# Graph attention scores: a2.W h taken from the W h product and spread by transposes, in place of a second product

## The chip, the cores and the metric

The kernel runs on one core of a Trainium2 chip. The core has five engines with instruction queues of their own that meet only in semaphores: PE (TensorE, matrix products and transposes into PSUM), DVE (VectorE), ACT (ScalarE), POOL (GpSimd) and SP (SyncE, DMA issue). The metric is the device time of one execution in microseconds; lower is better.

## The reference

A batch of 32 graphs with 256 nodes and 128 features passes two pre-norm blocks with residuals. The change is in the first, a graph attention layer:

```python
h = jnp.maximum(_layernorm(x, axis=-1), 0.0)
Wh = jnp.einsum('bnf,fo->bno', h, W)
a1, a2 = (a[:Fout, 0], a[Fout:, 0])
s1 = Wh @ a1
s2 = Wh @ a2
e = s1[:, :, None] + s2[:, None, :]
e = jnp.where(e >= 0, e, ALPHA * e)
e = jnp.where(adj_matrix[None] == 0, -jnp.inf, e)
attention = jax.nn.softmax(e, axis=-1)
h_prime = jnp.einsum('bij,bjo->bio', attention, Wh)
```

The second block (two graph convolutions, then LSTM steps over windows of 1 to 4 rows) is left as it is.

## The kernel before

Two graphs, four tiles of 128 nodes, make a pair; there are 16 pairs (`PAIRS`). Every engine has its own program, written by hand in a fixed order. In phase A, the attention layer, `ticks` calls `phase_a(t, ph, live)` once for each tick t on each engine, and `live(s)` holds where pair t - s exists; so a tick works on several pairs at different depths. I write q for pair t - 1 and give the steps short names:

- **W(q)**, PE L898: four products `hT` times `wext` into `psW`. `wext` holds 130 columns: 0.8 a1.W, the 128 columns of W, and -a1.W.
- **S(q)**, PE L902: one product of `wa2`, a 128x128 matrix whose columns are all a2.W, with `hT`: 512 columns in which every row holds a2.W h of each node. It goes to `psS` and signals `a_S`.
- **T(q+1)**, PE L908: four transposes of `v_norm` into `psT`.
- **A(q-3)**, PE L917: eight products of `pT` with `wh`, the attention's sum, into `psA`; signals `a_att`.
- **PT(q-2)**, PE L929: eight transposes of `prob` into `psPT`.
- ACT, in this order in a tick: `wh` (L467, the copy of `psW` out of PSUM, signals `a_wh`), `hT` (L474), `prob` (L481, four exponentials, which need `ebias`), `v_norm` (L448, four), `pT` (L490, the copy of `psPT`).
- DVE, in this order: a wait on `a_S`; `low` (L650) of pair q-1 and the first of four score passes of pair q over `psS` (L642); `ebias` (L654) of pair q-1; the other three L642; two `bn_stats` (L632); four score passes of pair q that take `wh`'s -a1 column (L674, signal `a_z`); the reciprocal of the attention's row sums (L681, waits on `a_att`); two more L632; four updates of `xs` (L688) of pair q-3, which signal `a_x1`.

`low` and `ebias` of pair q-1 do not read `psS`, but they stand behind the wait on `a_S` of pair q in DVE's program. A(q-2) overwrites `psA` and so waits on `a_x1` of pair q-3. In the first five ticks DVE also takes the statistics of x for later pairs (L594), and POOL (L357 to L366) turns them into the scale and shift that `v_norm` needs; `v_norm` of pair 6 waits for the last of these.

Phase B (graph convolutions) begins beside the last ticks of phase A; from then on PE runs mostly the products of L937, and the LSTM steps follow.

Of the kernel before, what the change touches and what calls it, by code (L numbers as in the profile page):

```python
# [5 lines left out]
def preln_gat_gcn_lstm_kernel(  # L6
# [24 lines left out]
    ALU = mybir.AluOpType  # L31
# [25 lines left out]
    with ctx:  # L57
# [25 lines left out]
        adj_neg = sb("adj_neg", [P, 2, N])  # L83
        adjT_hi = sb("adjT_hi", [P, 2, N], fp32r)
        adjT_lo = sb("adjT_lo", [P, 2, N], fp32r)
        wext = sb("wext", [P, D + 2])
        wa2 = sb("wa2", [P, P])
        wt = sb("wt", [P, D])
        a12 = sb("a12", [P, 2])
        wg_raw = sb("wg_raw", [P, 2, D])  # L90
# [27 lines left out]
        with ExitStack() as early:  # L118
            def sb_early(name, shape):
                return early.enter_context(nc.sbuf_tensor(name, shape, fp32))  # L120

            hT = sb_early("hT", [P, 512])
            score = sb_early("score", [P, 4, 4, N])
            prob = sb_early("prob", [P, 4, 4, N])
            pT = sb_early("pT", [P, 4, N])

            wh = sb_early("wh", [P, 4, 4, D + 3])
        h_hi = sb("h_hi", [P, NODES], fp32r)
        with ExitStack() as parts_end:
            h_lo = parts_end.enter_context(nc.sbuf_tensor("h_lo", [P, NODES], fp32r))  # L130
# [16 lines left out]

        ps = ctx.enter_context(nc.psum_tensor("ps", [P, 8, 512], fp32))
        psT = ps[:, 0, :]
        psW = ps[:, 1:3, 0:2 * (D + 2)]  # L150
        psS = ps[:, 3, :]
        psPT = ps[:, 4:6, :]
        psA = ps[:, 6:8, 0:2 * (D + 2)]
# [178 lines left out]
        def _(pool):  # L332
            n = 0

            def done(ins):
# [8 lines left out]
            done(nc.gpsimd.memset(ident[:, :], 0.0))  # L344
            nc.gpsimd.affine_select(out=ident[:, :], in_=ident[:, :], compare_op=ALU.not_equal, fill=1.0, base=0,
                                    pattern=[[-1, P]], channel_multiplier=1).then_inc(ident_ok, 1)
            nc.gpsimd.memset(wh[:, :, :, D + 2:D + 3], 1.0)
            nc.gpsimd.memset(ones[:, :].bitcast(fp32), 1.0).then_inc(ones_ok, 1)
            done(nc.gpsimd.memset(half[:, :], -0.5))

# [78 lines left out]
        def _(act):  # L429
            act.dma_start(wt[:, :], w_gat_t).then_inc(gat_w_in, 16)  # L430
            act.dma_start(a12[:, :], a_gat).then_inc(gat_w_in, 16)
            act.dma_start(wext[:, 1:D + 1], w_gat).then_inc(wext_in, 16)
            act.dma_start(adj_raw[:, :, :], adj.rearrange("(u p) n -> p u n", p=P)).then_inc(adj_in, 16)
            act.dma_start(adjT_raw[:, :, :], adj_t.rearrange("(u p) n -> p u n", p=P)).then_inc(adjT_in, 16)
            act.dma_start(wg_raw[:, 0], w_gcn0).then_inc(gcn_w_in, 16)
# [26 lines left out]
            def early_a(t, ph, live):  # L462
                if live(1):

                    act.wait_ge(a_W, t)
                    after(act, a_att, t - 4, 0)
                    nc.scalar.activation(  # L467
                        wh[:, (ph - 1) % 4, :, 0:D + 2].rearrange("p (b u) f -> p b u f", b=2),
                        psW.rearrange("p b (u f) -> p b u f", u=2), ACT.Copy).then_inc(a_wh, 1)
                if live(0):  # L470

                    act.wait_ge(a_T, t + 1)
                    after(act, a_S, t, 0)
                    nc.scalar.activation(hT[:, :], psT, ACT.Relu).then_inc(a_hT, 1)  # L474
                if live(2):

                    m = (ph - 2) % 4
                    act.wait_ge(a_bias, t - 1)
                    after(act, a_PT, t - 5, 0)
                    for k in range(4):  # L480
                        ins = nc.scalar.activation(prob[:, m, k], score[:, m, k], ACT.Exp, scale=1.0 - SLOPE,  # L481
                                                   bias=ebias[:, m, k:k + 1])
                    ins.then_inc(a_exp, 1)
# [96 lines left out]
        def _(dve):  # L580
# [16 lines left out]
            first_statistics(1, 0)  # L597

            dve.wait_ge(wa_ps, 1)
            nc.vector.tensor_scalar(wext[:, D + 1:D + 2], ps[:, 0, 0:1], -1.0, None, ALU.mult)  # L600
            nc.vector.tensor_scalar(wext[:, 0:1], ps[:, 0, 0:1], 1.0 - SLOPE, None, ALU.mult)
            nc.vector.tensor_copy(wa2[:, :], ps[:, 0, 1:2].to_broadcast([P, P])).then_inc(wa_ok, 1)
            first_statistics(2, 0)
            dve.wait_ge(adj_in, 16)
            done(nc.vector.tensor_scalar(adj_neg[:, :, :], adj_raw[:, :, :], 0.0, MASKED, ALU.is_equal, ALU.mult))
# [19 lines left out]
            def phase_a(t, ph, live):  # L625
                def statistics(k):

                    if live(5):
                        if k == 0:
                            dve.wait_ge(a_x1, (t - 5) * 2 + 2)  # L630
                        i = (t - 5) * 4 + k
                        nc.vector.bn_stats(stats[:, 1, bass.ds(i, 1), :].rearrange("p o s -> p (o s)"),  # L632
                                           xs[:, bass.ds(i, 1), :].rearrange("p o f -> p (o f)")
                                           ).then_inc(stats_ok, 1)

                for k in range(0):
                    statistics(k)

                def scores(k):

                    b, u, m = k // 2, k % 2, (ph - 1) % 4
                    return nc.vector.tensor_tensor_reduce(  # L642
                        out=score[:, m, k], in0=psS[:, b * N:(b + 1) * N], in1=adj_neg[:, u, :],
                        scale=SLOPE_RATIO, scalar=-3e38, op0=ALU.add, op1=ALU.max, accum_out=m2[:, m, k:k + 1])

                def row_maximum(k):

                    m = (ph - 2) % 4
                    if k == 0:
                        nc.vector.scalar_tensor_tensor(low[:, :], m2[:, m, :], -SLOPE / SLOPE_RATIO, wh[:, m, :, 0],  # L650
                                                       ALU.mult, ALU.add).then_inc(low_ok, 1)
                    elif k == 1:
                        dve.wait_ge(low_ok, t - 1)
                        nc.vector.scalar_tensor_tensor(ebias[:, m, :], m2[:, m, :], -1.0 / SLOPE_RATIO, low[:, :],  # L654
                                                       ALU.mult, ALU.min).then_inc(a_bias, 1)

                if live(1):
                    dve.wait_ge(a_S, t)
                for k in range(4):
                    if live(2):  # L660
                        row_maximum(k)
                    if live(1):
                        ins = scores(k)
                if live(1):
                    ins.then_inc(a_t, 1)
                for k in range(0, 2):
                    statistics(k)
                if live(1):

                    dve.wait_ge(a_wh, t)  # L670
                    dve.wait_ge(a_t, t)
                    for k in range(4):
                        m, b = (ph - 1) % 4, k // 2
                        ins = nc.vector.scalar_tensor_tensor(score[:, m, k], psS[:, b * N:(b + 1) * N],  # L674
                                                             wh[:, m, k, D + 1:D + 2], score[:, m, k], ALU.max, ALU.add)
                    ins.then_inc(a_z, 1)
                if live(4):

                    dve.wait_ge(a_att, t - 3)
                    pa = psA.rearrange("p b (u f) -> p b u f", u=2)  # L680
                    nc.vector.reciprocal(rinv[:, :].rearrange("p (b u) -> p b u", b=2),  # L681
                                         pa[:, :, :, D + 1]).then_inc(a_x1, 1)
                    for k in range(2, 4):
                        statistics(k)
                    dve.wait_ge(a_x1, (t - 4) * 2 + 1)
                    for k in range(4):
                        xt = xs[:, bass.ds((t - 4) * 4 + k, 1), :].rearrange("p o f -> p (o f)")
                        ins = nc.vector.scalar_tensor_tensor(xt, pa[:, k // 2, k % 2, 0:D], rinv[:, k:k + 1], xt,  # L688
                                                             ALU.mult, ALU.add)
                    ins.then_inc(a_x1, 1)  # L690
                else:
                    for k in range(2, 4):
                        statistics(k)
                if isinstance(t, int) and t == 1:
                    adj_parts()
                if isinstance(t, int) and t == 2:
                    row_sum_parts()
                if isinstance(t, int) and t < 5:
                    first_statistics((t + 5) // 2, (t + 1) % 2)
# [171 lines left out]
        def _(pe):  # L871
# [16 lines left out]
            def phase_a(t, ph, live):  # L888
# [4 lines left out]
                if live(1):  # L893
# [1 line left out]
                    pe.wait_ge(a_hT, t)  # L895
                    after(pe, a_wh, t - 1, 0)
                    for k in range(4):
                        ins = nc.tensor.matmul(psW[:, k // 2, (k % 2) * (D + 2):(k % 2 + 1) * (D + 2)],  # L898
                                               hT[:, k * P:(k + 1) * P], wext[:, :], start=True, stop=True)
                    ins.then_inc(a_W, 1)  # L900
                    after(pe, a_z, t - 1, 0)
                    nc.tensor.matmul(psS, wa2[:, :], hT[:, :], start=True, stop=True).then_inc(a_S, 1)  # L902
                if live(0):

                    pe.wait_ge(a_v, t + 1)
# [4 lines left out]
                if live(4):  # L910
# [3 lines left out]
                    for b in range(2):  # L914
                        for ui in range(2):
                            for uj in range(2):
                                ins = nc.tensor.matmul(psA[:, b, ui * (D + 2):(ui + 1) * (D + 2)],  # L917
                                                       pT[:, 2 * b + uj, ui * P:(ui + 1) * P],
                                                       wh[:, (ph - 4) % 4, 2 * b + uj, 1:D + 3],
                                                       start=(uj == 0), stop=(uj == 1))  # L920
                    ins.then_inc(a_att, 1)
                if live(3):

                    pe.wait_ge(a_exp, t - 2)
# [162 lines left out]
```

## Time and profile before

| | us |
|---|---|
| median of 3 runs | 476.65 (476.65 to 477.36) |
| profiled execution, its own time | 477.25 |
| its span, first to last instruction | 475.4 |
| PE busy in the span | 431.2 |
| DVE busy | 382.0 |
| ACT busy | 322.8 |
| POOL busy | 70.7 |

Busy time is the sum of an engine's instructions. A matmul's record overlaps the next one's, so the distance from one group's start to the next one's start is what a group takes of PE's time. The profile's column PEclk is the granted TensorE clock as a share of 2.4 GHz: 1.00 is 2.4 GHz, 0.50 is 1.2 GHz.

### The profile page before, as it was taken

How to read it: one execution, taken by the hardware profiler on the slowest of the kernel's cores; microseconds unless marked ns; L12 is line 12 of the kernel's file. 1: busy time of each engine (PE TensorE's matmuls, PEld its weight loads, DVE VectorE, ACT ScalarE, POOL GpSimd, SP SyncE). 2: the span in 40 equal slices, each digit the busy share in tenths (PEclk: the TensorE clock that was granted, in tenths of full speed). 3: DMA queues.
4: the chain of work that ended last, by engine and by line, in shares of the span. 5: the costliest groups of instructions: out<-in, count | busy, mean ns of one | idle time of the engine just before them, and what ended most of it. 6: DMA issues, size and time to landing. Idle time of an engine off the chain costs nothing.

```text
span 475.4 us, 8063 instructions
## 1 busy us (share of the span) xinstructions
PE 431.2 (91%) x2522; PEld 378.7 (80%) x2522; DVE 382.0 (80%) x985; ACT 322.8 (68%) x630; POOL 70.7 (15%) x163
## 2 busy tenths in 40 slices
PE   0659799997999899999989999999999999999971
PEld 0438688887999798999878888899999988888861
DVE  3599699997868977878777788888788788888883
ACT  0658699987687687887676677767667665585520
POOL 4614853304046500000000000000000000000000
PEclk9998799999999899999999999999999999999986
DMA  8900000000000000000000000000000000000038
GB/s 242 338 18 2 1 1 3 0 0 0 1 2 2 0 0 0 0 0 0 1 0 2 0 1 1 0 1 1 1 1 1 2 0 1 0 0 1 1 106 249
DMA packets 13994, 11.67 MB, mean 25 GB/s; under 512 B 902, under 2 KB 12172, under 8 KB 13708
## 3 DMA queue, kind: packets, MB, share of 16 engines
q1 hardware_dynamic: 8176, 8.39, 5.8%
q10 hardware_dynamic: 5788, 2.91, 2.3%
q8 instruction: 16, 0.26, 0.2%
q14 instruction: 14, 0.11, 0.1%
HBM read 7.10 MB, written 4.19 MB: 24 GB/s over the span
## 4 chain that ended last, share of the span: by engine, by line
PE 72%; DVE 15%; issue 4%; ACT 3%; POOL 2%; DMA 1%; DVEq 1%; ACTq 0%; POOLq 0%
PE ps L937 47%; PE ps L1036 12%; PE ps L1040 6%; DVE score L674 3%; DVE score L642 3%; PE ps L917 3%; DVE xs L688 2%; DVE stats L594 1%; ACT v_norm L448 1%; DVE stats L632 1%; POOL scale L363 1%; ACT work L550 1%; DMA xs<-in_x 1%; PE ps L1055 1%; PE ps L902 1%
## 5 line engine op out<-in xcount | busy, mean ns | idle before, releaser
L550 ACT ACTIVATE work<-ps,bl 128x512 f32<-128x512 f32 (+2 forms) x204 | 111.2, 628 | 26.7 <-PE ps L1040 20.0
L937 PE MATMUL ps<-h_hi,wl_hi 128*128 128x512 f32 (+3 forms) x252 | 94.2, 374 | 3.2 <-DVE h_lo L738 3.2
L937 PE MATMUL ps<-h_lo,wl_hi 128*128 128x512 f32 (+3 forms) x252 | 94.0, 373 | 0.0
L937 PE MATMUL ps<-h_hi,wl_lo 128*128 128x512 f32 (+3 forms) x252 | 93.9, 373 | 0.0
L540 ACT ACTIVATE work<-work 128x512 f32<-128x512 f32 (+2 forms) x56 | 31.5, 570 | 45.4 <-DVE work L822 34.5
L937 PEld LDWEIGHTS ps<-h_hi,wl_hi 128*128 128x128 f32 x252 | 47.5, 189 | 10.5 <-issue 2.0
L448 ACT ACTIVATE v_norm<-xs,shift,scale 128x128 f32 (+1 forms) x128 | 52.8, 492 | 3.9 <-POOL shift L366 3.9
L937 PEld LDWEIGHTS ps<-h_lo,wl_hi 128*128 128x128 f32 x252 | 47.7, 189 | 7.6
L937 PEld LDWEIGHTS ps<-h_hi,wl_lo 128*128 128x128 f32 x252 | 47.7, 189 | 6.8
L1036 PE MATMUL ps<-s_hi,wl_lo 128*128 128x512 f32 (+2 forms) x144 | 51.5, 360 | 0.0
L1036 PE MATMUL ps<-s_hi,wl_hi 128*128 128x512 f32 (+2 forms) x144 | 51.3, 358 | 0.0
L523 ACT ACTIVATE s_hi<-ps 128x512 fp32r<-128x512 f32 x48 | 28.4, 599 | 19.5 <-PE ps L937 16.1
L917 PE MATMUL ps<-wh,pT 128*128 128x130 f32 x256 | 35.6, 296 | 2.7 <-DVE xs L688 2.3
L917 PEld LDWEIGHTS ps<-wh,pT 128*128 128x128 f32 x256 | 32.9, 207 | 5.2 <-issue 2.3
L511 ACT ACTIVATE work<-ps,bl 128x512 f32<-128x512 f32 x48 | 30.9, 682 | 8.9 <-DVE work L712 7.0
L1040 PE MATMUL ps<-s_lo,wl_hi 128*128 128x512 f32 (+2 forms) x144 | 34.0, 358 | 0.3 <-DVE s_lo L784 0.3
L773 DVE TENSOR_TENSOR s_hi<-work 128x512 fp32r<-128x512 f32 (+2 forms) x36 | 22.0, 611 | 12.6 <-ACT work L540 11.8
L481 ACT ACTIVATE prob<-score,ebias 128x256 f32<-128x256 f32 x64 | 27.5, 520 | 5.8 <-DVE ebias L654 5.8
L777 DVE TENSOR_TENSOR work<-work 128x512 f32<-128x512 f32 (+2 forms) x52 | 31.2, 601 | 0.0
L1036 PEld LDWEIGHTS ps<-s_hi,wl_lo 128*128 128x128 f32 x144 | 27.1, 188 | 3.6
L1036 PEld LDWEIGHTS ps<-s_hi,wl_hi 128*128 128x128 f32 x144 | 27.1, 188 | 3.4
L736 DVE TENSOR_TENSOR s_lo<-ps,s_hi 128x512 fp32r<-128x512 f32 x32 | 21.9, 686 | 9.3 <-ACT s_hi L523 9.3
(127 smaller groups left out, 951.3 us busy)
## 6 DMA issues: line engine op xcount, KB each, us to landing
result<-xs SPq DMA_DIRECT2D x8, 256.0 KB, 4.4
result<-xs ACTq DMA_DIRECT2D x8, 256.0 KB, 4.9
xs<-in_x SPq DMA_DIRECT2D x2, 512.0 KB, 5.1
work<-in_w_ih_t SPq DMA_DIRECT2D x1, 1024.0 KB, 11.3
work<-in_w_hh_t SPq DMA_DIRECT2D x1, 1024.0 KB, 9.3
adj_raw<-in_adj ACTq DMA_DIRECT2D x1, 256.0 KB, 8.5
adjT_raw<-in_adj_t ACTq DMA_DIRECT2D x1, 256.0 KB, 10.0
wg_raw<-in_w_gcn ACTq DMA_DIRECT2D x2, 64.0 KB
```

What stands on the lines that cost most here:

```text
L448: ins = nc.scalar.activation(v_norm[:, k, :], xs[:, bass.ds(i, 1), :].rearrange("p o f -> p (o f)"), ACT.Relu, scale=scale[:, which, bass. ...
L481: ins = nc.scalar.activation(prob[:, m, k], score[:, m, k], ACT.Exp, scale=1.0 - SLOPE, bias=ebias[:, m, k:k + 1])
L511: nc.scalar.activation(one_row(g), ps[:, 4 + g, :], ACT.Tanh if g == G else ACT.Sigmoid, bias=bl[:, g:g + 1]).then_inc(one_act, 1)
L523: nc.scalar.activation(dst, ps[:, s - 1, :], ACT.Copy if s in (1, 3) else ACT.Relu).then_inc(b_hi[s], 1)
L540: nc.scalar.activation(lw[:, par, R_TC, 0:cols], lw[:, par, R_C, 0:cols], ACT.Tanh).then_inc(c_act[par], 1)
L550: nc.scalar.activation(lw[:, par, g, 0:cols], ps[:, 4 * par + g, 0:cols], ACT.Tanh if g == G else ACT.Sigmoid, bias=bl[:, (p - 1) * GATES ...
L773: nc.vector.tensor_tensor(hi, shaped(lw[:, par, O, :]), shaped(lw[:, par, R_TC, :]), ALU.mult).then_inc(c_hi[par], 1)
L777: nc.vector.tensor_tensor(row(r, par, R_H), row(r, par, O), row(r, par, R_TC), ALU.mult).then_inc(c_h[par], 1)
L917: ins = nc.tensor.matmul(psA[:, b, ui * (D + 2):(ui + 1) * (D + 2)], pT[:, 2 * b + uj, ui * P:(ui + 1) * P], wh[:, (ph - 4) % 4, 2 * b + u ...
L937: ins = nc.tensor.matmul(dst, a, b, start=start and n_ == 0, stop=stop and n_ == 2)
L1036: nc.tensor.matmul(ps[:, 4 * par + g, 0:cols], part, s_hi[:, par, 0:cols], start=False, stop=False)
L1040: nc.tensor.matmul(ps[:, 4 * par + g, 0:cols], weights(p, 1, g)[0], s_lo[:, par, 0:cols], start=False, stop=True).then_inc(c_gate[par], 1)
```

## The change

`wa2` goes. Its column becomes column 0 of `wext`, so that W(q) yields 131 columns, a2.W h among them; the columns of `wh` move by one. S(q) is now four transposes of `wh`'s column 0, read 128 times over (`to_broadcast`), one for each tile. Since they read `wh`, PE waits for ACT's copy (`a_wh`), and S(q) now stands behind A(q-3) in the tick. `hT` waits on `a_W` in place of `a_S`.

```diff
-        wext = sb("wext", [P, D + 2])
-        wa2 = sb("wa2", [P, P])
+        wext = sb("wext", [P, D + 3])
...
                     nc.scalar.activation(
-                        wh[:, (ph - 1) % 4, :, 0:D + 2].rearrange("p (b u) f -> p b u f", b=2),
+                        wh[:, (ph - 1) % 4, :, 0:D + 3].rearrange("p (b u) f -> p b u f", b=2),
...
                     act.wait_ge(a_T, t + 1)
-                    after(act, a_S, t, 0)
+                    after(act, a_W, t, 0)
                     nc.scalar.activation(hT[:, :], psT, ACT.Relu).then_inc(a_hT, 1)
...
-            nc.vector.tensor_copy(wa2[:, :], ps[:, 0, 1:2].to_broadcast([P, P])).then_inc(wa_ok, 1)
+            nc.vector.tensor_copy(wext[:, 0:1], ps[:, 0, 1:2]).then_inc(wa_ok, 1)
...
                     for k in range(4):
-                        ins = nc.tensor.matmul(psW[:, k // 2, (k % 2) * (D + 2):(k % 2 + 1) * (D + 2)],
+                        ins = nc.tensor.matmul(psW[:, k // 2, (k % 2) * (D + 3):(k % 2 + 1) * (D + 3)],
                                                hT[:, k * P:(k + 1) * P], wext[:, :], start=True, stop=True)
                     ins.then_inc(a_W, 1)
-                    after(pe, a_z, t - 1, 0)
-                    nc.tensor.matmul(psS, wa2[:, :], hT[:, :], start=True, stop=True).then_inc(a_S, 1)
...
                     ins.then_inc(a_att, 1)
+                if live(1):
+
+                    pe.wait_ge(a_wh, t)
+                    after(pe, a_z, t - 1, 0)
+                    for k in range(4):
+                        ins = nc.tensor.transpose(psS[:, k * P:(k + 1) * P],
+                                                  wh[:, (ph - 1) % 4, k, 0:1].to_broadcast([P, P]), ident[:, :])
+                    ins.then_inc(a_S, 1)
                 if live(3):
```

PE's rows of one full tick before the change, with what each waits for (W at L898, S at L902, T at L908, A at L917, PT at L929):

```order
L898 MATMUL ps<-wext,hT 128x130 [waits a_wh,a_hT]
L898 MATMUL ps<-wext,hT 128x130 x3
L902 MATMUL ps<-hT,wa 128x512 [waits a_z]
L908 MATMUL ps<-ident,v_norm 128x128 [waits a_hT,a_v]
L908 MATMUL ps<-ident,v_norm 128x128 x3
L917 MATMUL ps<-wh,pT 128x130 [waits a_x1,a_pT]
L917 MATMUL ps<-wh,pT 128x130 x7
L929 MATMUL ps<-ident,prob 128x128 [waits a_pT,a_exp]
L929 MATMUL ps<-ident,prob 128x128 x7
```

The same tick of the changed kernel (W is now at L897, T at L905, A at L914, S at L924, PT at L934):

```order
L897 MATMUL ps<-wext,hT 128x131 [waits a_wh,a_hT]
L897 MATMUL ps<-wext,hT 128x131 x3
L905 MATMUL ps<-ident,v_norm 128x128 [waits a_hT,a_v]
L905 MATMUL ps<-ident,v_norm 128x128 x3
L914 MATMUL ps<-wh,pT 128x130 [waits a_x1,a_pT]
L914 MATMUL ps<-wh,pT 128x130 x7
L924 MATMUL ps<-ident,wh 128x128 [waits a_z,a_wh]
L924 MATMUL ps<-ident,wh 128x128 x3
L934 MATMUL ps<-ident,prob 128x128 [waits a_pT,a_exp]
L934 MATMUL ps<-ident,prob 128x128 x7
```

S moved from ahead of T and A to behind both, and its first transpose waits for ACT's `wh` too.

The end of phase A on PE before the change, from the last W and S on (no T is left, and two A and two PT follow):

```order
L898 MATMUL ps<-wext,hT 128x130 x4
L902 MATMUL ps<-hT,wa 128x512
L917 MATMUL ps<-wh,pT 128x130 x8
L929 MATMUL ps<-ident,prob 128x128 x8
L917 MATMUL ps<-wh,pT 128x130 x8
L929 MATMUL ps<-ident,prob 128x128 x8
```

And of the changed kernel:

```order
L897 MATMUL ps<-wext,hT 128x131 x4
L914 MATMUL ps<-wh,pT 128x130 x8
L924 MATMUL ps<-ident,wh 128x128 x4
L934 MATMUL ps<-ident,prob 128x128 x8
L914 MATMUL ps<-wh,pT 128x130 x8
L934 MATMUL ps<-ident,prob 128x128 x8
```

The last S moved behind A(12); one A is left behind it beside the start of phase B.

## Rows read from the trace of the kernel before

**Rows 1.** The page, busy time (share of span) by engine

```profile
PE 431.2 (91%) x2522; PEld 378.7 (80%) x2522; DVE 382.0 (80%) x985; ACT 322.8 (68%) x630; POOL 70.7 (15%) x163
```

**Rows 2.** Windows, one full stretch of phase A: stretch, length, busy by engine, PEclk

```profile
75.00:80.00 5.00, 5.00 (x40) 4.34 (x39) 5.00 (x24) 5.00 (x12) 0.32 (x2) 1.00 0.02 7
```

**Rows 3.** Timeline of one tick of phase A: start, duration, engine

```profile
85.37 0.60 PE L908 MATMUL ps<-ident,v_norm 128*128 128x128 f32 x4
...
85.57 0.17 DVE L650 SCALAR_TENSOR_TENSOR low<-m,wh 128x4 f32<-128x4 f32 x1
...
85.87 2.06 PE L917 MATMUL ps<-wh,pT 128*128 128x130 f32 x16
...
86.00 0.16 DVE L654 SCALAR_TENSOR_TENSOR ebias<-m,low 128x4 f32<-128x4 f32 x1
...
86.56 1.74 ACT L481 ACTIVATE prob<-score,ebias 128x256 f32<-128x256 f32 x4
...
87.77 1.04 PE L929 MATMUL ps<-ident,prob 128*128 128x128 f32 x8
88.16 1.69 ACT L448 ACTIVATE v_norm<-xs,shift,scale 128x128 f32 x4
...
88.64 1.06 PE L898 MATMUL ps<-wext,hT 128*128 128x130 f32 x8
...
89.52 1.11 DVE L688 SCALAR_TENSOR_TENSOR xs<-ps,rinv,xs 128x128 f32 x4
89.53 1.02 PE L902 MATMUL ps<-hT,wa 128*128 128x512 f32 x2
89.70 1.05 ACT L490 ACTIVATE pT<-ps 128x1024 f32<-128x1024 f32 x1
...
90.59 0.17 DVE L650 SCALAR_TENSOR_TENSOR low<-m,wh 128x4 f32<-128x4 f32 x1
```

**Rows 4.** Timeline around the first A and the first S behind it

```profile
35.12 1.66 DVE L674 SCALAR_TENSOR_TENSOR score<-ps,wh,score 128x256 f32<-128x256 f32 x4
...
36.84 1.12 PE L902 MATMUL ps<-hT,wa 128*128 128x512 f32 x2 [3.93 <-DVE score L674]
37.16 1.00 ACT L490 ACTIVATE pT<-ps 128x1024 f32<-128x1024 f32 x1
...
38.25 0.15 DVE L650 SCALAR_TENSOR_TENSOR low<-m,wh 128x4 f32<-128x4 f32 x1
```

**Rows 5.** Timelines of PE, DVE and ACT up to pair 6

```profile
38.61 3.24 PE L917 MATMUL ps<-wh,pT 128*128 128x130 f32 x16
...
43.14 1.63 DVE L594 BATCH_NORM_STATS2 stats<-xs 128x6 f32<-128x128 f32 x8
...
51.02 1.65 ACT L448 ACTIVATE v_norm<-xs,shift,scale 128x128 f32<-128x128 f32 x4 [3.89 <-POOL shift L366]
...
52.72 1.12 PE L908 MATMUL ps<-ident,v_norm 128*128 128x128 f32 x4 [3.30 <-ACT v_norm L448]
53.63 3.83 PE L917 MATMUL ps<-wh,pT 128*128 128x130 f32 x16
```

**Rows 6.** Timeline of DVE, the L650 behind the last S

```profile
105.63 0.17 DVE L650 SCALAR_TENSOR_TENSOR low<-m,wh 128x4 f32<-128x4 f32 x1
```

**Rows 7.** Timeline of PE behind its later pauses

```profile
110.83 2.03 PE L917 MATMUL ps<-wh,pT 128*128 128x130 f32 x16 [2.11 <-DVE xs L688]
...
156.57 0.50 PE L937 MATMUL ps<-h_hi,wl_hi 128*128 x1 [1.81 <-DVE h_lo L738]
```

**Rows 8.** Windows of the stretches behind these pauses, columns as in Rows 2

```profile
51.50:54.90 3.40, 2.18 (x10) 1.99 (x11) 0.95 (x4) 3.40 (x9) 3.04 (x9) 0.50 0.01 2
...
110.00:120.00 10.00, 8.81 (x71) 8.45 (x72) 7.10 (x27) 7.46 (x16) 4.76 (x10) 1.00 0.00 0
...
157.30:160.70 3.40, 3.40 (x11) 2.72 (x11) 3.37 (x6) 1.70 (x3) 3.16 (x5) 0.50 0.00 0
```

**Rows 9.** Windows of L1055's transposes alone: length, PE, PEld, PEclk

```profile
457.70:461.00 3.30, 3.15 (x14) 2.75 (x15) 0.50 0.56 164
461.10:464.50 3.40, 3.37 (x28) 2.72 (x26) 1.00 1.01 283
```

More of the change, by code:

```diff
@@ L125, in preln_gat_gcn_lstm_kernel @@
             pT = sb_early("pT", [P, 4, N])
-            wh = sb_early("wh", [P, 4, 4, D + 3])
+            wh = sb_early("wh", [P, 4, 4, D + 4])
         h_hi = sb("h_hi", [P, NODES], fp32r)
@@ L149, in preln_gat_gcn_lstm_kernel @@
         psT = ps[:, 0, :]
-        psW = ps[:, 1:3, 0:2 * (D + 2)]
+        psW = ps[:, 1:3, 0:2 * (D + 3)]
         psS = ps[:, 3, :]
@@ L346, in _ @@
                                     pattern=[[-1, P]], channel_multiplier=1).then_inc(ident_ok, 1)
-            nc.gpsimd.memset(wh[:, :, :, D + 2:D + 3], 1.0)
+            nc.gpsimd.memset(wh[:, :, :, D + 3:D + 4], 1.0)
             nc.gpsimd.memset(ones[:, :].bitcast(fp32), 1.0).then_inc(ones_ok, 1)
@@ L431, in _ @@
             act.dma_start(a12[:, :], a_gat).then_inc(gat_w_in, 16)
-            act.dma_start(wext[:, 1:D + 1], w_gat).then_inc(wext_in, 16)
+            act.dma_start(wext[:, 2:D + 2], w_gat).then_inc(wext_in, 16)
             act.dma_start(adj_raw[:, :, :], adj.rearrange("(u p) n -> p u n", p=P)).then_inc(adj_in, 16)
@@ L599, in _ @@
             dve.wait_ge(wa_ps, 1)
-            nc.vector.tensor_scalar(wext[:, D + 1:D + 2], ps[:, 0, 0:1], -1.0, None, ALU.mult)
-            nc.vector.tensor_scalar(wext[:, 0:1], ps[:, 0, 0:1], 1.0 - SLOPE, None, ALU.mult)
-            nc.vector.tensor_copy(wa2[:, :], ps[:, 0, 1:2].to_broadcast([P, P])).then_inc(wa_ok, 1)
+            nc.vector.tensor_scalar(wext[:, D + 2:D + 3], ps[:, 0, 0:1], -1.0, None, ALU.mult)
+            nc.vector.tensor_scalar(wext[:, 1:2], ps[:, 0, 0:1], 1.0 - SLOPE, None, ALU.mult)
+            nc.vector.tensor_copy(wext[:, 0:1], ps[:, 0, 1:2]).then_inc(wa_ok, 1)
             first_statistics(2, 0)
@@ L649, in row_maximum @@
                     if k == 0:
-                        nc.vector.scalar_tensor_tensor(low[:, :], m2[:, m, :], -SLOPE / SLOPE_RATIO, wh[:, m, :, 0],
+                        nc.vector.scalar_tensor_tensor(low[:, :], m2[:, m, :], -SLOPE / SLOPE_RATIO, wh[:, m, :, 1],
                                                        ALU.mult, ALU.add).then_inc(low_ok, 1)
@@ L674, in phase_a @@
                         ins = nc.vector.scalar_tensor_tensor(score[:, m, k], psS[:, b * N:(b + 1) * N],
-                                                             wh[:, m, k, D + 1:D + 2], score[:, m, k], ALU.max, ALU.add)
+                                                             wh[:, m, k, D + 2:D + 3], score[:, m, k], ALU.max, ALU.add)
                     ins.then_inc(a_z, 1)
@@ L918, in phase_a @@
                                                        pT[:, 2 * b + uj, ui * P:(ui + 1) * P],
-                                                       wh[:, (ph - 4) % 4, 2 * b + uj, 1:D + 3],
+                                                       wh[:, (ph - 4) % 4, 2 * b + uj, 2:D + 4],
                                                        start=(uj == 0), stop=(uj == 1))
                     ins.then_inc(a_att, 1)
+                if live(1):
[5 more added lines that the diff above has]
+                    ins.then_inc(a_S, 1)
                 if live(3):
```

## The prediction

> **What bounds the kernel now.** I began with busy time by engine: PE leads with 431.2 us of the span, DVE follows with 382.0 [rows 1]. That is a mean over stages, and the change touches phase A alone, so the next view was busy time in a stretch of phase A. From 75 to 80 us PE, DVE and ACT are all three busy for 5.00 of 5.00 us, with the granted clock at 1.00 [rows 2]. Then I read one tick in the timeline [rows 3]. The reader is to see two things there. First, it repeats after 5.02 us (L650 at 85.57 and at 90.59), and each of the three engines fills it with its own work: no single wait is the bound, and a saving on PE alone has nowhere to go. Second, who starts whom. L650 starts 0.04 us after S ends (89.53 + 1.02 = 90.55, then 90.59): S is what lets DVE into its tick. Now S(q+1) needs only W(q+1) and DVE's L674 of pair q; the long work A and PT of the same tick is not between DVE's tick q and S(q+1) through any semaphore that S waits for.
>
> **What PE saves.** S took 1.02 us, and 0.86 of PE's time before the change (89.53 to 90.39 by the recurring start of L908, which lies 5.02 behind 85.37) [rows 3]. Four transposes of this size take 0.60 with the drain of the last, or about 0.44 of PE's time: L929's eight take 0.87 (87.77 to 88.64) [rows 3]. That the transposed operand is one column read over and over has no row; its bounds are the four plain transposes (0.60) and the old product (1.02), and I take 0.60, the same operation and shape. W grows by one column in 130, under 0.01 us of 0.89. So PE's work falls by about 0.43 us in each of 16 ticks, 6.9 in all. It comes to nothing: DVE and ACT cover it, since both are full already [rows 2]. The shorter copy of a2.W on DVE before the first tick and the four more elements in `wh` are nothing as well, at most some ten ns a tick.
>
> **What the new place costs.** S(q+1) now stands behind A(q-2) on PE. A(q-2) waits for `a_x1` of pair q-3, which is the very last thing in DVE's tick q; and DVE's tick q begins with S(q). So a ring closes over one tick that went over two before:
>
> - S(q) ends, L650 starts: 0.04 [rows 3]
> - DVE's tick from L650 to the end of L688: 89.52 + 1.11 - 85.57 = 5.06 [rows 3]
> - DVE's signal to PE: 36.84 - (35.12 + 1.66) = 0.06 [rows 4]
> - A(q-2), start to the next group's start: 87.77 - 85.87 = 1.90 [rows 3]
> - S(q+1), four transposes: 0.60 [rows 3]
>
> The sum is **7.66 us** a tick against 5.02. ACT has a ring that is nearly as long: L650 to the end of L654 0.59 (86.00 + 0.16 - 85.57), 0.06 to `prob` (as DVE's signal to PE), 1.60 for `prob` (86.56 to 88.16), 1.54 for `v_norm` (88.16 to 89.70), 1.05 for `pT`, then 0.06, A 1.90, S 0.60 and 0.04: 7.44 [rows 3]. So a shorter DVE tick alone would gain 0.22. The wait on `a_wh` that the diff adds costs nothing more: `wh` follows `pT` on ACT and is ready while A runs.
>
> Queued behind the late S are PT(q-2) and W(q+1), 0.87 and 0.89 us, and the whole DVE tick; ACT's `prob` is late through `ebias`. What falls idle is PE: 4.6 us of work in 7.66.
>
> **Summed over phase A.** S(0) to S(2) have no A ahead of them; they go on waiting for `wh` or for L674 as S(3) does [rows 4], so they cost nothing. S(3) is the first behind an A.
>
> 1. `pT` of pair 0 ends at 38.16 [rows 4], so A(0) starts at 38.2. It starts at half clock, as before the change, where its record took 3.24 us [rows 5]; S follows at 41.4 and L650 at 42.0. It was at 38.25 [rows 4]: **+3.8**.
> 2. In this DVE tick stand the statistics for the last x tiles, whose end (43.14 + 1.63 = 44.77) lies 6.52 behind that L650; from there to `v_norm` of pair 6 it is 6.25 (51.02), POOL's chain, and 2.61 more to A(2) at 53.63 [rows 4, 5]. T(6) and A(2) now stand ahead of S(5). After that long pause A(2) ran at half clock, 3.83 instead of 2.06, so 3.67; S at half clock 1.1. L650 behind S(5) comes at 42.0 + 6.52 + 6.25 + 2.61 + 3.67 + 1.1 + 0.04 = 62.2.
> 3. From S(5) to S(15) are ten ticks of 7.66: 138.8. The kernel before was there at 105.63 [rows 6]: **+33.2**, with 3.8 of it from step 1.
> 4. Behind S(15) all follows L650 as before. But PE has only PT(13) to do until A(13), some 4 us of pause instead of 2.11 [rows 7]. If the clock falls there, A(13) and what follows cost up to 1.7 more; I take 1.3.
>
> **The clock.** At half clock A costs 3.83 - 2.06 = 1.77 more and S about 0.5, the difference of 1.12 and 0.60 that four transposes show [rows 3, 5]: up to 2.25 in a tick. In the new tick W ends 1.6 us behind L650 (PT 0.87 and W 0.89 behind S) and T waits for `v_norm`, which ends at 0.59 + 0.06 + 1.60 + 1.69 = 3.9 [rows 3]: PE pauses for about 2.4 us, does T, and pauses 0.7 again, just ahead of A. In this trace the clock stood at 0.50 behind pauses of 3.93, 3.30 and even 1.81 us, and at 1.00 behind one of 2.11 [rows 4, 5, 7, 8]. The new pauses lie among these, so the trace bounds the term between 0 and 10 x 2.25 = 22.5 and does not decide; I take the middle, half the price in each tick, **+11.5**.
>
> The Trainium skill ("TensorE: Matmul & The Clock Gate", Part 4: PE-mode transpose) says that the full clock doesn't engage for transposes, which don't count as busy in the same way. By it a change from products to transposes would leave PE at half clock in these thinner ticks, and the sum would have the full 22.5. The row beside it: behind 3.30 us with nothing but L1055's transposes at 0.50, the next stretch, transposes again, is at 1.00 [rows 9]. Here the trace speaks against the page, so I keep the middle.
>
> The sum is 33.2 + 1.3 + 11.5 = 46 us, on the profiled execution's own 477.25: 523. The median lies 0.6 below that execution, which I leave inside the rounding. A measurement of this kernel can tell about 0.2%, 1 us, from no change.
>
> **The rivals.**
>
> - *The clock stays at 1.00 through the ring.* For it: the pause of 2.11 that left it full, and the new pauses are split by T. Against it: the fall behind 1.81 [rows 7, 8]. The sum without the clock term is 33 to 34, **511**. Chance 17%.
> - *Half clock in all ticks.* A tick is then 7.66 + 2.25 = 9.91, with some 9.1 us of PE work in it, so PE would hardly pause at all; that is against it, as a fully busy stretch at 0.50 was followed by 1.00 [rows 9]. The Trainium skill's rule above speaks for it. The sum is 477.25 + 33.2 + 1.7 + 22.5 = **535**. Chance 11%.
> - *Faster or no change: PE sets the beat and S's place is free.* PE is the busiest engine, and 0.43 us less a tick is 6.9 in all. It holds if DVE's tick q can end while A(q-2) is still ahead, that is, if DVE runs a tick ahead of PE. Then ACT's and DVE's own 4.97 to 5.00 us a tick would be the floor, and the time about 476 to 477. Against it: DVE cannot be ahead, since its wait on `a_S` is the first thing in its tick and A(q-2) waits for the tick's last signal. It would decide as soon as the ring were under 5.0, and it is 2.6 over. Chance 3%.
> - *The ring is shorter than I read*, because one of its links overlaps the next (A may start on `psA` or S be answered earlier). Half the growth, 1.3 a tick, gives 477 + 3.8 + 9 + 13 = 503 with a little of the clock. Chance 4%.
>
> **How the numbers follow.** The forecast, ring of 7.66 with the clock falling in a part of the ticks, has 65% and gives 523, within 514 to 531. The range reaches down toward the clean clock and up to nearly the half clock: 508 to 534, which leaves out the short ring, the no-change case and about the outer part of both clock cases, under 2 in 10. Faster by over 0.2% gets 0.02, within it 0.01, slower 0.97.
>
> **What the changed profile would show.** Right: L650 to L650 at 7.6 to 9 us in the middle of phase A; PE with pauses there that end on `v_norm` and on L688; DVE idle for about 2.5 us a tick, ended by the transposes; ACT idle ahead of `prob`; `wh` not the releaser of S; PEclk below 1.00 in part of phase A; everything from the second phase on as before, only later. The transposes of `wh` at about 0.11 us apart would confirm their price. Wrong: DVE without idle time in phase A, or a tick near 5. Most likely to spoil the number is the clock, and next the transposes of a repeated column, if they are slow: 0.4 more would add 0.4 in each of 12 ticks, 5 us.

## The result, and the profile after

The changed kernel takes 517.71 us (median of 4 runs, 516.72 to 518.60) against 476.65 before (476.56 to 477.36): 1.0857 times as long, 95% interval 1.0833 to 1.0882. The profiled execution took 517.27, its span is 515.4 against 475.4. The forecast was 523, its range 508 to 534. The ratios further on stand against runs of the kernel before that were taken beside each experiment; their medians are 477.17 and 477.18.

The page first, busy time by engine, the answer to [rows 1]:

```profile
PE 439.0 (85%) x2554; PEld 392.3 (76%) x2554; DVE 382.4 (74%) x985; ACT 323.5 (63%) x630; POOL 71.2 (14%) x163
```

DVE and ACT have the work they had. PE's sum even rose by 7.8, though it has less to do: more of its work ran at half clock (the mean granted clock of the execution is 0.953, before it was 0.974). For DVE and ACT the 40 us are waits. The timeline of the changed kernel over one tick at full clock, L649 to L649, the answer to [rows 3]:

```profile
102.42 0.16 DVE L649 SCALAR_TENSOR_TENSOR low<-m,wh 128x4 f32<-128x4 f32 x1 [4.24 <-PE ps L924]
...
104.35 1.64 DVE L673 SCALAR_TENSOR_TENSOR score<-ps,wh,score 128x256 f32<-128x256 f32 x4
104.73 1.63 ACT L447 ACTIVATE v_norm<-xs,shift,scale 128x128 f32 x4
...
106.27 1.01 ACT L489 ACTIVATE pT<-ps 128x1024 f32<-128x1024 f32 x1
106.37 1.11 DVE L687 SCALAR_TENSOR_TENSOR xs<-ps,rinv,xs 128x128 f32 x4
106.42 0.66 PE L905 MATMUL ps<-ident,v_norm 128*128 128x128 f32 x4 [2.26 <-ACT v_norm L447]
107.17 0.59 ACT L466 ACTIVATE wh<-ps 128x524 f32<-128x524 f32 x1
107.54 2.05 PE L914 MATMUL ps<-wh,pT 128*128 128x130 f32 x16 [0.46 <-DVE xs L687]
...
109.43 0.60 PE L924 MATMUL ps<-ident,wh 128*128 128x128 f32 x4
109.86 1.04 PE L934 MATMUL ps<-ident,prob 128*128 128x128 f32 x8
110.06 0.17 DVE L649 SCALAR_TENSOR_TENSOR low<-m,wh 128x4 f32<-128x4 f32 x1 [2.58 <-PE ps L924]
...
110.68 1.71 ACT L480 ACTIVATE prob<-score,ebias 128x256 f32<-128x256 f32 x4 [2.44 <-DVE ebias L653]
```

Read it as a ring. L687 ends at 107.48; A (L914) starts at 107.54; the next group on PE, the transposes of `wh`, at 109.43, 1.89 later; they end at 110.03; L649 starts at 110.06. The L649 before stands at 102.42, so this tick took 7.64. `wh` (L466) was ready at 107.76, long before its transposes. The brackets show who waits: DVE 2.58 us for the transposes, ACT 2.44 for `ebias`, PE for `v_norm` and then for L687.

The waits of the changed kernel from 60 to 140 us (engine and line, what it waited for, us in total, times, longest) show the same in sum:

```profile
DVE low L649 <- PE ps L924: 34.9, 10, 5.1
ACT prob L480 <- DVE ebias L653: 33.0, 10, 4.3
```

And the timeline of PE in the tick before that one, where the clock had fallen:

```profile
97.04 0.66 PE L905 MATMUL ps<-ident,v_norm 128*128 128x128 f32 x4 [2.18 <-ACT v_norm L447]
98.24 3.57 PE L914 MATMUL ps<-wh,pT 128*128 128x130 f32 x16 [0.54 <-DVE xs L687]
101.61 0.78 PE L924 MATMUL ps<-ident,wh 128*128 128x128 f32 x4
```

A's record took 3.57 instead of 2.05 and L924 0.78 instead of 0.60. The windows of these stretches (length, then busy us of PE, PEld, DVE, ACT and POOL, then the granted clock) give the levels:

```profile
98.60:101.90 3.30, 3.30 (x18) 3.30 (x17) 0.00 (x0) 0.27 (x1) 0.00 (x0) 0.50 0.00 0
102.00:105.30 3.30, 2.15 (x20) 1.96 (x18) 2.88 (x15) 2.18 (x6) 0.00 (x0) 1.00 0.00 0
```

The steps of L649 that the prediction named are in DVE's timeline, behind S(3), S(5) and S(15); the line at 93.13 opens the tick with the fallen clock, which ends at 102.42:

```profile
41.85 0.17 DVE L649 SCALAR_TENSOR_TENSOR low<-m,wh 128x4 f32<-128x4 f32 x1 [3.50 <-PE ps L924]
...
60.96 0.23 DVE L649 SCALAR_TENSOR_TENSOR low<-m,wh 128x4 f32<-128x4 f32 x1 [5.12 <-PE ps L924]
...
93.13 0.17 DVE L649 SCALAR_TENSOR_TENSOR low<-m,wh 128x4 f32<-128x4 f32 x1 [2.58 <-PE ps L924]
...
144.94 0.17 DVE L649 SCALAR_TENSOR_TENSOR low<-m,wh 128x4 f32<-128x4 f32 x1 [3.55 <-PE ps L924]
```

At 144.94 the kernel is 39.3 us behind the one before (105.63, [rows 6]), of the 40.0 by which the whole span grew.

PE's timeline has A(2) and S(5) ahead of the L649 at 60.96, and then A(13), the first A behind S(15):

```profile
56.88 3.20 PE L914 MATMUL ps<-wh,pT 128*128 128x130 f32 x16 [0.25 <-ACT pT L489]
59.87 1.06 PE L924 MATMUL ps<-ident,wh 128*128 128x128 f32 x4
...
150.15 3.48 PE L914 MATMUL ps<-wh,pT 128*128 128x130 f32 x16 [3.61 <-DVE xs L687]
```

### The profile page after: what moved, and what is told of

It is laid out like the page before. It is cut to its first block, busy times and chain, and to the rows that moved or that the text cites. A ratio compares the mean times of both kernels' runs of the same rounds, so it can differ in the third digit from the quotient of the medians.

```text
span 515.4 us, 8142 instructions
## 1 busy us (share of the span) xinstructions
PE 439.0 (85%) x2554; PEld 392.3 (76%) x2554; DVE 382.4 (74%) x985; ACT 323.5 (63%) x630; POOL 71.2 (14%) x163
## 4 chain that ended last, share of the span: by engine, by line
PE 72%; DVE 16%; issue 3%; ACT 3%; POOL 2%; DMA 1%; DVEq 1%; ACTq 0%; POOLq 0%
PE ps L942 44%; PE ps L1041 11%; PE ps L914 7%; PE ps L1045 5%; DVE score L673 4%; DVE score L641 3%; DVE xs L687 2%; PE ps L924 2%; ACT v_norm L447 1%; DVE stats L631 1%; DVE stats L593 1%; POOL scale L362 1%; ACT work L549 1%; DMA xs<-in_x 1%; PE ps L1060 1%
## 5 line engine op out<-in xcount | busy, mean ns | idle before, releaser
L942 PE MATMUL ps<-h_hi,wl_hi 128*128 128x512 f32 (+3 forms) x252 | 94.2, 374 | 3.2 <-DVE h_lo L737 3.2
L942 PE MATMUL ps<-h_lo,wl_hi 128*128 128x512 f32 (+3 forms) x252 | 94.0, 373 | 0.0
L942 PE MATMUL ps<-h_hi,wl_lo 128*128 128x512 f32 (+3 forms) x252 | 93.9, 373 | 0.0
L942 PEld LDWEIGHTS ps<-h_hi,wl_hi 128*128 128x128 f32 x252 | 47.6, 189 | 10.5 <-issue 2.0
L914 PE MATMUL ps<-wh,pT 128*128 128x130 f32 x256 | 43.3, 338 | 12.6 <-DVE xs L687 12.1
L942 PEld LDWEIGHTS ps<-h_lo,wl_hi 128*128 128x128 f32 x252 | 47.7, 189 | 7.6
L942 PEld LDWEIGHTS ps<-h_hi,wl_lo 128*128 128x128 f32 x252 | 47.7, 189 | 6.9
L914 PEld LDWEIGHTS ps<-wh,pT 128*128 128x128 f32 x256 | 39.7, 243 | 16.0 <-issue 7.9
L905 PE MATMUL ps<-ident,v_norm 128*128 128x128 f32 x64 | 11.8, 314 | 38.7 <-ACT v_norm L447 38.7
L905 PEld LDWEIGHTS ps<-ident,v_norm 128*128 128x128 f32 x64 | 7.7, 156 | 41.4 <-ACT v_norm L447 34.7
L649 DVE SCALAR_TENSOR_TENSOR low<-m,wh 128x4 f32<-128x4 f32 x16 | 2.7, 167 | 44.6 <-PE ps L924 44.6
```

Source lines behind the costliest of these rows:

```text
L942: ins = nc.tensor.matmul(dst, a, b, start=start and n_ == 0, stop=stop and n_ == 2)
```

## The experiments

The theory: the place of S behind A closes a ring (S, DVE's tick, A, S), and the clock falls in the pauses that the ring leaves on PE. The rivals: the transposes or their wait for `wh` cost by themselves; the late `ebias` does it, through ACT; the clock is the cause and not a consequence.

**1. The old product, behind A.** The kernel before with its two lines of S moved; no transposes, no wait for `wh`. ACT's `hT` still waits on `a_S` here, which the change replaced by `a_W`.

```diff
-                    after(pe, a_z, t - 1, 0)
-                    nc.tensor.matmul(psS, wa2[:, :], hT[:, :], start=True, stop=True).then_inc(a_S, 1)
...
                     ins.then_inc(a_att, 1)
+                if live(1):
+                    after(pe, a_z, t - 1, 0)
+                    nc.tensor.matmul(psS, wa2[:, :], hT[:, :], start=True, stop=True).then_inc(a_S, 1)
```

> The kernel before, with its a2.W product as it was and no wait on wh, but issued behind A instead of ahead of T. My theory (the place of S closes a ring S, DVE's tick, A, S): a tick grows to 7.66 + 0.42 = 8.1 us, since the product with its drain takes 1.02 where four transposes take 0.60, and with the clock falling at times the time is 515 to 526 us. Rival one (the cost lies in the transposes or in waiting for wh): about 477 us, DVE without idle time. Rival two (the falling clock is the cause, not the place): near 477 as well, as PE has as much work as before.

Measured: 527.16 us (524.93 to 529.39), ratio 1.1061 (1.1031 to 1.1092). PE's and then DVE's timeline of this kernel:

```profile
103.30 2.06 PE L915 MATMUL ps<-wh,pT 128*128 128x130 f32 x16 [0.54 <-DVE xs L688]
105.20 1.02 PE L922 MATMUL ps<-hT,wa 128*128 128x512 f32 x2
...
98.19 0.17 DVE L650 SCALAR_TENSOR_TENSOR low<-m,wh 128x4 f32<-128x4 f32 x1 [4.67 <-PE ps L922]
106.26 0.17 DVE L650 SCALAR_TENSOR_TENSOR low<-m,wh 128x4 f32<-128x4 f32 x1 [3.01 <-PE ps L922]
```

A tick at full clock is 8.07 us (98.19 to 106.26), the 8.08 of the sum. The time is 1 us over the expected range. The clock fell in seven of the ten ticks from S(5) to S(15), and a tick in which it fell took 9.6 to 9.8; in the changed kernel it fell in five. The place alone costs more than the whole change did: the transposes, being shorter, make the ring 0.43 shorter. Rival one is out: with the product and no wait for `wh` the loss is there. So is rival two in the form given, since PE has its old amount of work. The clock falls here too, though; what speaks against it as the cause is the full-clock tick of 8.07, and experiment 4.

**2. The transposes ahead of A.** The changed kernel with the block of four transposes moved up between T and A.

```diff
+                if live(1):
+
+                    pe.wait_ge(a_wh, t)
+                    after(pe, a_z, t - 1, 0)
...
                 if live(4):
 
                     pe.wait_ge(a_pT, t - 3)
```

> The changed kernel with the four transposes issued between T and A, waiting for wh. My theory: DVE's tick is out of the ring again, and what is left is ACT's ring S, ebias, prob, v_norm, pT, wh, S: 0.04 + 0.59 + 0.06 + 1.60 + 1.54 + 0.90 + 0.63 + 0.06 + 0.60 = 6.0 us a tick, 1.0 more than before in 10 to 12 ticks: 487 to 491 us, little or no half clock. Rival (transposes of a repeated column or the wait on wh cost by themselves, wherever they stand): near 517 us.

Measured: 487.62 us (486.85 to 488.01), ratio 1.0214 (1.0194 to 1.0235). Its timeline:

```profile
104.03 0.59 ACT L466 ACTIVATE wh<-ps 128x524 f32<-128x524 f32 x1
...
104.67 0.65 PE L912 MATMUL ps<-ident,wh 128*128 128x128 f32 x4 [0.74 <-ACT wh L466]
105.16 1.95 PE L922 MATMUL ps<-wh,pT 128*128 128x130 f32 x16
105.36 0.17 DVE L649 SCALAR_TENSOR_TENSOR low<-m,wh 128x4 f32<-128x4 f32 x1 [0.94 <-PE ps L912]
...
105.98 1.71 ACT L480 ACTIVATE prob<-score,ebias 128x256 f32<-128x256 f32 x4 [0.88 <-DVE ebias L653]
...
111.36 0.17 DVE L649 SCALAR_TENSOR_TENSOR low<-m,wh 128x4 f32<-128x4 f32 x1 [0.94 <-PE ps L912]
```

A tick is 6.00 here (105.36 to 111.36), as the sum of ACT's ring has it (6.02). Three quarters of the 41 us are gone with the same transposes and the same wait, and the clock's share with them: from 60 to 120 us the granted clock is 1.00. The rest is a second ring, and here the wait for `wh` is in it: PE stands 0.74 us for L466.

**3. S behind A, `ebias` early.** The changed kernel; DVE computes `low` and `ebias` of pair q-1 ahead of the wait on `a_S`.

```diff
+                if live(2):
+                    row_maximum(0)
+                    row_maximum(1)
                 if live(1):
                     dve.wait_ge(a_S, t)
+                    if live(2):
+                        nc.vector.scalar_tensor_tensor(rinv[:, :], m2[:, (ph - 2) % 4, :], 1.0, low[:, :],
+                                                       ALU.mult, ALU.add)
                 for k in range(4):
-                    if live(2):
-                        row_maximum(k)
```

> The changed kernel, S behind A, but DVE computes low and ebias of pair q-1 ahead of its wait on a_S (one small extra operation of 4 elements carries the wait). This takes ACT's prob out of the ring and leaves DVE's tick in it. My theory (DVE's ring of 7.66 binds, ACT's of 7.44 is just shorter): a tick of 7.5 to 7.7 us, 512 to 519 us in all. Rival (the late ebias, and so ACT's ring, is what the change costs): a tick near 5, 480 us or less.

Measured: 515.30 us (514.35 to 517.18), ratio 1.0802 (1.0769 to 1.0835): within 2.4 us of the changed kernel. In its timeline the extra operation, which now carries the wait on `a_S`, has DVE's line L662:

```profile
103.00 0.16 DVE L662 SCALAR_TENSOR_TENSOR rinv<-m,low 128x4 f32<-128x4 f32 x1 [3.27 <-PE ps L928]
...
108.04 2.05 PE L918 MATMUL ps<-wh,pT 128*128 128x130 f32 x16 [2.16 <-DVE xs L691]
108.29 1.70 ACT L480 ACTIVATE prob<-score,ebias 128x256 f32<-128x256 f32 x4 [1.61 <-DVE ebias L653]
...
110.57 0.16 DVE L662 SCALAR_TENSOR_TENSOR rinv<-m,low 128x4 f32<-128x4 f32 x1 [2.31 <-PE ps L928]
```

From L662 to L662 it is 7.57, a tick at full clock. PE no longer waits for `v_norm` ahead of T; the whole pause stands ahead of A and ends on DVE's L691. So ACT was not what set the tick, as the 0.22 between the two rings said, and freeing ACT moves the pause without shortening it.

**4. The pause filled.** The changed kernel with 16 transposes whose results nothing uses.

```diff
+                if live(4) and live(0):
+
+                    for k in range(16):
+                        nc.tensor.transpose(psT[:, (k % 4) * P:(k % 4 + 1) * P], ident[:, :], ident[:, :])
```

> The changed kernel with 16 transposes of the identity into psT, results unused, between W and T in each tick that has an A and a T: 1.75 us of PE work in the pause of 2.2. They are extra work for PE and nothing waits for them. My theory (part of the cost is TensorE's clock at 0.50 during A and S behind the pause): the granted clock stays at 1.00 from about S(5) on, each tick is 7.65, and the time falls by 6 to 9 us against the changed kernel, 508 to 511 us. Rival (transposes don't count for the clock, as the Trainium skill's page TensorE: Matmul & The Clock Gate says in its part 4): the clock falls as before and the time stays at 517 us or above.

Measured: 510.48 us (510.22 to 511.22), ratio 1.0701 (1.0682 to 1.0721). More work on PE makes the kernel 7.2 us faster. The windows over nine ticks of it, and then over nine ticks of the changed kernel (L649 at 60.96 and at 136.34), and DVE's timeline at the two ends of the filled ones:

```profile
60.00:128.80 68.80, 59.88 (x506) 55.63 (x505) 45.54 (x207) 46.12 (x99) 16.64 (x42) 1.00 0.00 1
```

```profile
61.00:137.00 76.00, 51.55 (x368) 47.71 (x367) 46.26 (x212) 46.16 (x100) 16.76 (x42) 0.91 0.00 1
```

```profile
60.00 0.17 DVE L649 SCALAR_TENSOR_TENSOR low<-m,wh 128x4 f32<-128x4 f32 x1 [6.78 <-PE ps L928]
...
128.84 0.16 DVE L649 SCALAR_TENSOR_TENSOR low<-m,wh 128x4 f32<-128x4 f32 x1 [2.58 <-PE ps L928]
```

The nine ticks take 7.65 each (60.00 to 128.84), at a clock of 1.00 throughout, where the changed kernel has a mean of 0.91. Nine ticks take 75.38 us there and 68.84 here: the clock's share of them is 6.5 us. The 7.2 between the medians also holds 1.0 gained ahead of S(5) and 0.8 lost in the tenth tick, which has no filling (no T is left): there the clock fell here too. So the clock is some 7 of the 41 us. It also shows which is cause: with the clock at full all through this stretch the ticks still take 7.6, so the clock comes on top of the ring.

**5. Both rings opened.** The block of experiment 2 and the edit of experiment 3 together, and as a control that edit alone on the kernel before.

> The transposes between T and A as in the second experiment, and DVE's low and ebias ahead of its wait on a_S as in the third. Neither DVE's tick nor ACT's is in a ring over one tick any more. My theory: phase A falls back to what the engines' own work sets, 5.0 us on ACT and 4.97 plus 0.1 for the small extra operation on DVE: a tick of 5.0 to 5.15 us, 476 to 480 us in all, so PE's saved 0.43 us a tick brings nothing. Rival (PE set the beat before, so its saved time shows as soon as no ring is in the way): about 471 us.

> The kernel before with only DVE's low and ebias ahead of its wait on a_S, as a control for the two experiments with this edit. My theory: no ring over one tick is there to be opened, and DVE's tick grows by the small extra operation, 0.0 to 0.1 us in 10 ticks: 477 to 479 us. Rival (the late ebias held the kernel before as well): 475 us or less.

Measured: 482.72 us (482.04 to 483.20), ratio 1.0117 (1.0095 to 1.0138), and for the control 481.35 us (479.47 to 482.20), ratio 1.0074 (1.0052 to 1.0095). Both are over what I expected. The control's timeline shows a part of the reason:

```profile
88.16 0.15 DVE L650 SCALAR_TENSOR_TENSOR low<-m,wh 128x4 f32<-128x4 f32 x1
...
88.35 0.16 DVE L654 SCALAR_TENSOR_TENSOR ebias<-m,low 128x4 f32<-128x4 f32 x1
...
88.45 0.16 DVE L663 SCALAR_TENSOR_TENSOR rinv<-m,low 128x4 f32<-128x4 f32 x1
88.53 0.42 DVE L642 CUSTOM_DVE_ANT_0 score<-ps,adj_neg 128x256 f32<-128x256 f32 x1
...
93.35 0.15 DVE L650 SCALAR_TENSOR_TENSOR low<-m,wh 128x4 f32<-128x4 f32 x1
```

A tick is 5.19. Three small dependent operations now stand alone for 0.37 us where L642 used to lie between them, and DVE was full. I had priced the extra operation at 0.1 and forgotten the latency that the old order covered. That is 0.2 a tick, and less than half of the excess. The control's span is 5.0 us over the one before; 1.7 of it had come by the end of S(6), 1.4 came in the nine ticks from there to S(15), and 1.9 behind, where A(13) ran for the most part at half clock, 3.46 behind a pause of 2.26, against 2.03 behind 2.11 before [rows 7]:

```profile
114.32 3.46 PE L921 MATMUL ps<-wh,pT 128*128 128x130 f32 x16 [2.26 <-DVE xs L692]
```

What the pair does say: opening both rings takes the transposes from 517.7 to 482.7, 1.4 us from a control that has no transposes.

**6. `ebias` in its own tick.** A reordering without an extra operation: `low` behind the first L674 pass, `ebias` behind the fourth, one `bn_stats` ahead of L642 to carry the wait on `a_S`, and ACT's `prob` waits on `a_z` too. Once with the transposes ahead of A, once with the old product.

```diff
+                    act.wait_ge(a_z, t - 1)
                     act.wait_ge(a_bias, t - 1)
...
+                statistics(0)
                 for k in range(4):
-                    if live(2):
-                        row_maximum(k)
                     if live(1):
                         ins = scores(k)
...
+                        if k == 0:
+                            row_maximum(0)
                     ins.then_inc(a_z, 1)
+                    row_maximum(1)
```

> The transposes between T and A, and DVE computes low and ebias of pair q in pair q's own tick, behind its last L641 and L674 passes, so that prob no longer hangs on the next S. The wait on a_S is carried by bn_stats, which moves ahead of the L641 passes: no operation is added and no latency laid bare, unlike in the early-bias kernels, where a tick was 5.2 to 5.4. My theory (DVE's 4.97 and ACT's 5.00 of work then set the tick): 5.0 to 5.15 us a tick and 473 to 478 us; the end of phase A may gain 1 to 3 us, since prob of the last pair need not wait for phase B's first DVE work. Rival (PE's wait for wh between T and A binds): 5.3 us a tick, 479 us or more.

> The kernel before, product and its place unchanged, with the same reordering of DVE's low, ebias and bn_stats. It tells what of the last kernel's time is the reordering and what the transposes. My theory: PE's 5.02 sets the tick as before, and only the end of phase A gains: 473 to 477 us. If the transposes are worth anything once no ring is in the way, this one is slower than its sibling by up to 0.02 us a tick, nothing measurable. Rival (the saved PE time has a value): this one is slower by 2 us or more.

Measured: 480.97 us (480.63 to 481.80), ratio 1.0075 (1.0059 to 1.0090), and with the product 480.13 us (477.55 to 482.07), ratio 1.0053 (1.0019 to 1.0086). The hoped for gain at the end of phase A did not show in either. With the transposes, `low` to `low` in DVE's timeline is 5.3 and 5.5:

```profile
79.79 0.15 DVE L650 SCALAR_TENSOR_TENSOR low<-m,wh 128x4 f32<-128x4 f32 x1
85.08 0.16 DVE L650 SCALAR_TENSOR_TENSOR low<-m,wh 128x4 f32<-128x4 f32 x1
90.58 0.15 DVE L650 SCALAR_TENSOR_TENSOR low<-m,wh 128x4 f32<-128x4 f32 x1
```

The rival on PE's wait for `wh` was given 5.3 and 479 or more, and those numbers came. But the sibling with the product, which has no such wait, missed its 5.02 as well. Its timeline of DVE:

```profile
87.54 0.16 DVE L651 SCALAR_TENSOR_TENSOR low<-m,wh 128x4 f32<-128x4 f32 x1
...
90.59 0.29 DVE L633 BATCH_NORM_STATS2 stats<-xs  x1 [0.15 <-DVE xs L690]
...
92.75 0.16 DVE L651 SCALAR_TENSOR_TENSOR low<-m,wh 128x4 f32<-128x4 f32 x1
```

A tick is 5.21 there. `bn_stats`, now first in the tick, waits 0.15 for the last update of `xs` just ahead of it on DVE itself, a wait that `low` and L642 used to cover. So the reordering did lay a latency bare, against what I expected of it. Over eight ticks the mean is 5.28 with the transposes (`low` at 69.25 and 111.50) and 5.22 with the product (66.57 and 108.34): most of the excess over 5.02 is the reordering, and at most 0.06 a tick is left for the wait for `wh`. The product kernel is not slower than its sibling, so PE's saved 0.43 us a tick bought nothing measurable there either; in every version with the transposes the saving comes together with the wait for `wh`, and no run has the one without the other. No version tried beats the kernel before.

## Why the prediction was right

The forecast held: slower, by 41 us where 46 were forecast, through the ring that it had named.

- **What PE saves** came as said. L924's four transposes take 0.60, with 0.43 to the start of L934 (109.43 to 109.86): reading one column over and over costs no more than a plain transpose. That the saving is worth nothing was right here: it lies where PE waits.
- **The ring** of 7.66 was measured at 7.64 in full-clock ticks, and at 7.65 through nine filled ticks. Experiments 1 and 2 move only S, the one in the kernel before and the other in the changed one, and get 8.07 and 6.00, where sums of the same kind give 8.08 and 6.02. Experiment 3 shows that DVE's ring binds and ACT's lies beneath it.
- **The wait on `wh` costs nothing**: so it is with S behind A (`wh` ends 1.67 us ahead of L924). With S ahead of A it is not so, experiment 2.
- **Step 1, S(3)**: the L650 behind it (now L649) at 42.0 forecast, 41.85 measured.
- **Step 2, S(5)**: 62.2 forecast, 60.96 measured. A(2) started at 56.88, 0.5 earlier than the 57.4 of the sum, and took 2.99 to the start of S, not 3.67, since its first part ran at full clock. S(5) took 1.06, all at half clock, as forecast (1.1).
- **Step 3**: ten ticks took 83.98, where 76.6 is the ring.
- **The clock** is the term that was mis-sized. I took half the price in each of ten ticks, 11.5 (half of 22.5 is 11.25). Measured is 83.98 - 76.6 = 7.4. It fell in five of the ten ticks, so the half was met, but not by any reasoning: the sum had left the term open between 0 and 22.5 and took the middle, and experiment 1 has seven such ticks of ten. That was luck. What was wrong is the price of a fall: four of the ticks were 1.5 to 1.7 longer (93.13 to 102.42 is 9.29) and the fifth, which has no T, 0.9, not 2.25. In none of them did the half clock cover all of A and S: A's record took 2.51 to 3.57, never 3.83, and in three of them S took 0.78 to 0.98, not the full 1.06.
- **Step 4, the end**: 1.3 forecast, 40.0 - 39.3 = 0.7 measured. The step itself came as described: behind a pause of 3.61, A(13) ran for the most part at half clock, 3.48 instead of 2.03. In the first products with `wg_hi` as weights (L942, before L937) the lag is 40.6 (163.41 against 122.80), 1.3 more than behind S(15); 0.6 of it is gone again by the end, and where is not taken apart.

So 33.2 + 1.3 + 11.5 = 46 reads 31.9 + 0.7 + 7.4 = 40.0 with what was measured. The ring, 32 of the 40, is what the forecast had right by reasoning. Its range of 508 to 534 took in nearly every state of the clock, so that the time fell inside it says little about the clock term. The rival "the clock stays at 1.00" was put at 511; it did not come about, and experiment 4, which brings it about for nine ticks, took 510.5. Why the clock falls in one tick and not in the next one like it, no run shows.

## What to carry to other kernels

Before moving an operation in an engine's program, ask what now stands ahead of it and what that waits for. Here a shorter operation was put behind one that waits for the last step of the very tick that the operation starts, and a dependence spread over two ticks became a ring over one. Add the ring up from durations in the timeline: the sum was right to 0.02 us in the three kernels where it was tried. When PE has pauses, price them at both clock levels. And when an operation is moved to the front of a tick, look at what it waits for on its own engine: that is what the two reorderings had left out. Where three engines are full in the same stretch, as here, time saved on one brings nothing until the others are shorter too.

## What the runs showed of the hardware that was not expected

Transposes kept the clock up. In experiment 4 the pause behind W holds nothing but fp32 transposes (L903), and over 68.8 us the granted clock stands at 1.00, where it had been 0.91 with the pause empty. The sentence of the Trainium skill weighed in the prediction ("TensorE: Matmul & The Clock Gate", Part 4: PE-mode transpose), that transposes don't count as busy in the same way, does not hold for them: by it the clock would have fallen as before.

A pause of 2.11 left the clock at 1.00 in the kernel before, and one of 2.26 in the same place was followed by an A mostly at half clock in the control of experiment 5 (2.03 against 3.46). The length of the pause alone does not tell: in the changed kernel pauses of 2.2 us stand ahead of ticks of both kinds.

Executions of one and the same program can lie 4 us apart. The product kernel of experiment 6 has three runs of 477.55 to 478.33 with a mean granted clock of 0.974 to 0.980, and three of 481.94 to 482.07 with 0.967. Which stretch makes the difference is not shown; only one run, of 477.55, has a trace.
